# A ViT tower with sparse attention and a product-key FFN: the FFN over one row of tokens in steps of 256, its hot columns, weights and rows all built on VectorE

## The reference

```python
q = (x @ Wq + bq).reshape(-1, N_HEADS, D_KEYS)          # 8 heads, two halves of 64
s1 = jnp.einsum('bhc,hnc->bhn', q1, keys[:, 0])          # 64 keys a half
s1t, i1 = lax.top_k(s1, TOP_K)                           # TOP_K = 8, and the same for s2
all_scores = s1t[..., :, None] + s2t[..., None, :]       # 8 x 8 pairs
scores, best = lax.top_k(all_scores, TOP_K)
indices = take_along_axis(i1 * 64 + i2, best)            # 8 of 4096 experts a head
inner = einsum('bd,bhkd->bhk', x, w_down[indices])
vals = relu(inner) * softmax(scores)
out = einsum('bhk,bhkd->bd', vals, w_up[indices])
```

## Time and profile before

| | us |
|---|---|
| median of 3 runs | 11114.34 (11099.82 to 11156.61) |
| profiled execution, its own time | 11131.57 |
| its span, first to last instruction | 11129.7 |
| mean granted TensorE clock | 0.746 of full |

### The profile page before, as it was taken

How to read it: one execution, slowest core, us unless ns; L and a number is a source line. 1 busy time by engine, 2 the same in 40 slices (tenths; PEclk the granted TensorE clock), 3 DMA queues, 4 the chain that set the end, 5 groups by cost and what they waited for, 6 DMA issues and landing times. The chain is left out here.

```text
span 11129.7 us, 231365 instructions
## 1 busy us (share of the span) xinstructions
PE 8355.6 (75%) x80373; PEld 6346.6 (57%) x80373; DVE 7817.8 (70%) x28721; ACT 3211.1 (29%) x6909; POOL 3313.1 (30%) x2904
## 2 busy tenths in 40 slices
PE   7777767776777677772777777688888888888883
PEld 7555545554555455552555554577777777777773
DVE  2555545555555455557999998888888888888983
ACT  0333333333333333332444444111111111111110
POOL 0111111111111111113444444344444444444441
PEclk8777767776777677776888888677777777777776
DMA  5333333333222333330000000000000000000000
GB/s 154 36 36 36 36 39 36 36 36 39 34 32 33 39 36 36 36 36 2 1 1 1 1 1 1 21 2 2 2 2 2 2 2 2 2 2 2 2 2 24
DMA packets 308211, 234.82 MB, mean 21 GB/s; under 512 B 34770, under 2 KB 305909, under 8 KB 306904
## 3 DMA queue, kind: packets, MB, share of 16 engines
q1 hardware_dynamic: 307224, 222.91, 14.5%
HBM read 48.28 MB, written 6.49 MB: 5 GB/s over the span
## 5 line engine op out<-in xcount | busy, mean ns | idle before, releaser
L1643 POOL TENSOR_TENSOR f_hotp<-f_hotc,f_part 128x1152 bf16<-128x1152 bf16 x579 | 1610.2, 2812 | 1557.0 <-DVE f_hotc L1555 1529.3
L617 DVE TENSOR_REDUCE negmax<-PAIR 99x4 f32<-99x788 f32 x1088 | 1064.5, 978 | 1191.6 <-PE PAIR L373 1052.2
L373 PE MATMUL PAIR<-ks,qs 96*99 96x198 bf16 x4352 | 815.2, 329 | 673.8 <-DVE negmax L617 565.3
L373 PEld LDWEIGHTS PAIR<-ks,qs 96*99 96x99 bf16 x4352 | 540.4, 167 | 1105.7 <-DVE negmax L617 864.6
L528 ACT ACTIVATE probs<-PAIR 99x792 f32<-99x792 f32 x1024 | 851.0, 831 | 1022.5 <-PE PAIR L383 1021.8
L1385 PE MATMUL f_OT<-f_act,f_wu 128*128 128x198 f32 x4096 | 865.5, 378 | 74.9 <-DVE f_act L1581 74.9
L1364 PE MATMUL f_AA<-f_hotp,f_hot 64*128 64x32 bf16 x19584 | 656.2, 236 | 310.3 <-DVE f_act L1581 257.4
L1385 PEld LDWEIGHTS f_OT<-f_act,f_wu 128*128 128x128 f32 x4096 | 831.8, 223 | 83.2 <-DVE f_act L1581 83.2
L383 PE MATMUL PAIR<-qs,ks 99*99 99x198 bf16 x4096 | 765.6, 329 | 124.9 <-ACT probs L528 107.4
L1364 PEld LDWEIGHTS f_AA<-f_hotp,f_hot 64*128 64x128 bf16 x19584 | 626.4, 161 | 342.0 <-DVE f_act L1581 270.0
L1563 DVE TENSOR_TENSOR f_hot<-f_idx,f_iota 128x4608 bf16<-128x4608 bf16 x193 | 804.5, 4168 | 0.0
(11 more groups left out here) (180 smaller groups left out, 15498.6 us busy)
## 6 DMA issues: line engine op xcount, KB each, us to landing
qs<-parts SPq DMA_DIRECT2D x816, 99.0 KB, 4.4
ks<-parts SPq DMA_DIRECT2D x816, 99.0 KB, 6.0
xbuf<-x_in SPq DMA_DIRECT2D x64, 588.0 KB, 4.4
qs<-mrows SPq DMA_DIRECT2D x272, 9.3 KB
out<-h SPq DMA_DIRECT2D x1, 3168.0 KB
out<-h SPq DMA_DIRECT2D x1, 3104.0 KB
wts<-layer_in SPq DMA_DIRECT2D x4, 772.0 KB, 4.2
f_wd<-wdown_in SPq DMA_DIRECT2D x1, 2048.0 KB, 11.0
```

What stands on the lines that cost most here:

```text
L373: mm = nc.tensor.matmul(ps[:, hh, qc * W:qc * W + W], qs[0:STACK, par, 2 * p + hh, j, qc * C:qc * C + C], ks[0:STACK, par, 2 * p + hh, j, ...
L617: V.tensor_reduce(negmax[:, j, :, 2 * p:2 * p + 2].rearrange("p q h -> p h q"), ps[:, :, 0:2 * W].rearrange("p h (q k) -> p h q k", q=2)[: ...
L1643: nc.gpsimd.tensor_tensor(hotp[:, g % 2, pt], hotc[:, g % 2], part[:, pt:pt + 1, t0:t0 + TG].to_broadcast([128, NP, TG]), ALU.mult).then_i ...
```

## The change

The FFN no longer works on h image by image but on one row of 12,672 tokens in DRAM, in 50 steps of 256 (two halves of 128 partitions); the last step begins earlier so that it ends with the row. Attention stores each image to it when it is done (new DMAs on SP's queue); each step loads its 256 rows twice (hx for the statistics and the normalisation, hr for the addition) and stores the sum straight to out. The four stores at the end are gone. h is freed before the FFN, and f_act is double. Four groups of 32 tokens and eight units of 16 replace the groups of 36; VectorE builds hotc (one buffer), all three parts of hotp in one instruction, and hot; GpSimd keeps only deviations. ScalarE normalises. The projection has the tokens as its stationary side, so that its result is in rows and the transposes back are gone; it is in two halves and lies in the next step. inner for the next step lies in pieces between the units of weights; the scores for the step after next likewise, through one PSUM bank (WK), which z and the columns share. In weights the two halves c are now innermost.

```diff
 build_attention, SyncE
+            for n in range(B):
+                upto(sp, added, n, 1)
+                to = tokens[n * W:n * W + W, :]
+                sp.dma_start(to[2:first, :], h[:, n, 0, :]).then_inc(tokens_stored, 16)
+                sp.dma_start(to[first:W, :], h[0:W - first, n, 1, :]).then_inc(tokens_stored, 16)
+                for slot, row in ((C - 2, 1), (C - 1, 0)):
+                    sp.dma_start(to[row:row + 1, :], h[slot:slot + 1, n, 1, :]).then_inc(tokens_stored, 16)
+            sp.wait_ge(tokens_stored, 64 * B)
 build_ffn
-TG = 36
-GROUPS = ((0, 32), (32, 64), (64, C))
+TP = 128
+STEP = 2 * TP
+TG = 32
+GROUPS = TP // TG
 UNIT = 16
+UNITS = TP // UNIT
+    NS = -(-T // STEP)
+    NS += NS % 2
+    at = [min(STEP * n, T - STEP) for n in range(NS)]
...
+        def steps(eng):
+            for n in range(2):
+                yield n, 0, n, n + 1 < NS, n + 2 < NS, n > 0
+            if NS > 4:
+                with eng.Fori(1, NS // 2 - 1) as it:
+                    for par in range(2):
+                        yield it * 2 + par, it, par, True, True, True
+            for n in range(max(NS - 2, 2), NS):
+                yield n, n // 2, n % 2, n + 1 < NS, n + 2 < NS, True
 SyncE
+            def load_x(n):
+                if n >= 2:
+                    upto(sp, z_done, n - 2, 1)
+                    upto(sp, mv_done, n - 2, 1)
+                sp.dma_start(hx[:, n % 2], rows(tokens, n)).then_inc(hx_loaded[n % 2], 16)
+            def load_r(n):
+                if n >= 2:
+                    sp.wait_ge(stored[n % 2], 16 * (n // 2))
+                sp.dma_start(hr[:, n % 2], rows(tokens, n)).then_inc(hr_loaded[n % 2], 16)
...
+            for n in range(NS):
+                load_r(n)
+                if n + 2 < NS:
+                    load_x(n + 2)
+                if n:
+                    store(n - 1)
 TensorE
+            def turn_cols(fr, behind):
+                upto(pe, s_taken, behind, 4)
                 upto(pe, cols_done, fr, 1)
...
+            def weights(n, u):
+                g, slot = u // 2, u % 2
                 upto(pe, hot_done, n, g + 1)
+                upto(pe, aa_taken[slot], n, u // 2)
+                for t in range(UNIT):
+                    tt = slot * UNIT + t
+                    for pt in range(3):
                         for c in range(2):
-                            for pt in range(3):
...
+            def project(n, par, c):
+                if c == 0:
                     for i in range(2):
                         upto(pe, aa_taken[i], n, aa_taken[i].per)
                     upto(pe, added, n, 0)
+                for k in range(NP):
+                    mm = nc.tensor.matmul(OT[:, c * DIM:c * DIM + DIM], act_in[:, par, k, c * TP:c * TP + TP], wu[:, k, :],
+                                          start=(k == 0), stop=(k == NP - 1))
...
+            for n, pair, par, has1, has2, behind in steps(pe):
+                for u in range(UNITS):
+                    if behind and u < 2:
+                        project(n - 1, 1 - par, u)
+                    weights(n, u)
+                    if has2:
+                        if u == 2:
+                            turn_z(n + 2)
+                        elif 3 <= u < 7:
+                            scores(n + 2, par, u - 3)
+                    if has1 and u == UNITS - 1:
+                        turn_cols(n + 1, n + 2 if has2 else n + 1)
+                    if has1 and u >= 2:
+                        first = (0, 2, 5, 8, 10, 13, 16)
+                        inner(n + 1, 1 - par, range(first[u - 2], first[u - 1]))
+            project(NS - 1, (NS - 1) % 2, 0)
+            project(NS - 1, (NS - 1) % 2, 1)
 VectorE
+            def hot_group(n, par, g):
+                t0 = g * TG
+                upto(dve, hotp_done, n, g)
+                V.tensor_tensor(hotc[:, 0], idx[:, par, 1:2, t0:t0 + TG].to_broadcast([128, NP, TG]), iota[:, 0:NP, :],
+                                ALU.is_equal).then_inc(hotc_done.sem, 1)
                 if g >= 2:
+                    upto(dve, aa_ready[1], n, g - 1)
+                elif not isinstance(n, int) or n > 0:
+                    upto(dve, aa_ready[1], n - 1, g + 3)
+                dve.sem_inc(spare, 1)
+                upto(dve, hotc_done, n, g + 1)
+                V.tensor_tensor(hotp[:, g % 2], hotc[:].to_broadcast([128, 3, NP, TG]),
+                                part[:, par, :, t0:t0 + TG].rearrange("p (k o) t -> p k o t", o=1).to_broadcast([128, 3, NP, TG]),
+                                ALU.mult).then_inc(hotp_done.sem, 1)
+                V.tensor_tensor(hot[:, g % 2], idx[:, par, 0:1, t0:t0 + TG].to_broadcast([128, 128, TG]), iota[:],
                                 ALU.is_equal).then_inc(hot_done.sem, 1)
```

More of the change, by code:

```diff
@@ L1193, in build_ffn @@
[L1193 to L1213, removed]
+        hx = sb("f_hx", [TP, 2, 2, DIM])
@@ L1214, in build_ffn @@
+        esum = sb("f_esum", [TP, 2, SEG])
+        idx = sb("f_idx", [128, 2, 2, TP], BF16)
+        part = sb("f_part", [128, 2, 3, TP], BF16)
+        rest = sb("f_rest", [128, 2, TP])
+        hotc = sb("f_hotc", [128, 1, NP, TG], BF16)
+        WK = bank("f_WK")
         IN = [bank(f"f_IN{i}") for i in range(2)]
-        AA = [bank(f"f_AA{i}") for i in range(2)]
+        AA = [[bank(f"f_AA{s}{c}") for c in range(2)] for s in range(2)]
         OT = bank("f_OT")
-        BK = OT[:, 256:512]
@@ L1225, in build_ffn @@
+        hr_loaded = [sem(f"f_hr_loaded{p}") for p in range(2)]
+        stored = [sem(f"f_stored{p}") for p in range(2)]
         dve_step = Count(sem("f_dve_step"), 16)
@@ new lines, in weigh @@
+            def weigh(n, par, u):
+                slot, t0 = u % 2, u * UNIT
+                if u == 0:
+                    upto(dve, inner_taken, n, NP // 2)
+                upto(dve, aa_ready[slot], n, u // 2 + 1)
+                for c in range(2):
+                    sl = act_in[:, par, :, c * TP + t0:c * TP + t0 + UNIT]
+                    last = V.tensor_tensor(sl, sl, AA[slot][c][:].rearrange("p (t n) -> p n t", n=NP), ALU.mult)
+                last.then_inc(aa_taken[slot].sem, 1)
@@ new lines, in _ @@
+            best_keys(0, 0)
+            met(0)
+            key_numbers(0, 0, segs)
+            pair_up(0)
+            for stage in (best_pairs, pair_numbers, ranks):
+                stage(0)
+            numbers_at_ranks(0, 0)
+            add_up(0, 0)
+            places(0)
+            split_cols(0, 0)
+            hot_group(0, 0, 0)
+            assert n_step[0] == dve_step.per, n_step
+            for n, pair, par, has1, has2, behind in steps(dve):
+                fr, other = n + 1, 1 - par
+                if has2:
+                    dve.wait_ge(hx_loaded[par], pair * 16 + 32)
+                    statistics(n + 2, par)
+                hot_group(n, par, 1)
+                if has1:
+                    best_keys(fr, other)
+                weigh(n, par, 0)
+                if has1:
+                    met(fr)
+                    key_numbers(fr, other, segs[:16])
+                weigh(n, par, 1)
+                hot_group(n, par, 2)
+                if behind:
+                    dve.wait_ge(hr_loaded[other], pair * 16 + 16 * par)
+                    add_back(n - 1, other)
+                if has1:
+                    key_numbers(fr, other, segs[16:])
+                    pair_up(fr)
+                weigh(n, par, 2)
+                if has1:
+                    best_pairs(fr)
+                weigh(n, par, 3)
+                hot_group(n, par, 3)
+                if has2:
+                    copy_scores(n + 2, par, 0)
+                if has1:
```

488 lines of the change are left out of this document (226 added, 262 removed).

## The result

| | before | changed |
|---|---|---|
| median, us | 11127.33 (4 runs, 11099.82 to 11156.61) | 10595.88 (4 runs, 10547.1 to 10633.82) |
| ratio, 95% interval | | 0.952 (0.9464 to 0.9575) |
| profiled execution, its span | 11131.57, 11129.7 | 10547.1, 10545.3 |

The account below looks back on a forecast made before the run. VectorE was taken to bound the old loop, TensorE close behind. Steps between 67.9 and 77.1 us were set at 73; 7177 + 48 x 73 gave span 10,681, then + 2 - 17 = 10,665 us, 4.0% faster; range 10,370 to 10,960.

Parts of the forecast that it names:

- VectorE's hot groups: VectorE building f_hotc, f_hotp and f_hot, four groups a step: 4.7 us each, 18.8 together.
- VectorE's sum: All VectorE work in a step of 256 rows, own pauses included: 61.2 us.
- the head: Step's start, through weighing unit 1 at 28.8 us: VectorE has 22.1 us of work and waits 6.7 for TensorE.
- The restart: TensorE's idle at the FFN loop's restart, 3.83 us every second step: 1.9 us a step.
- Small matmuls: TensorE's 96 weights matmuls a unit: 3.15 us, 25.2 for eight units, no effect from alternating halves; ends 12.4 either way.
- The rival on faster alternating matmuls: In weights, alternating halves hide half the weight load: 1.55 us less a unit, about 10,275 us; chance 0.15.
- The clock: TensorE's clock in the FFN loop falls at about every second unit; step between 67.9 (high) and 77.1 us (low).
- P: Period of one FFN step: 73 us expected, between 67.9 and 77.1; span = 7177 + 48 P.
- The bound: FFN step: VectorE bounds at 67.9 us if TensorE's clock stays high; low all through, TensorE's work makes it 77.1.
- A score bank passed back and forth: Single PSUM bank for scores exchanged between TensorE and VectorE: named with the clock's falls for 73 us, no separate price.
- Stores and frame: Start and end around the loop: 166 us of final stores go, one 128 KB store remains; span = 7177 + 48 P.
- the rival on the stores: Steps gain nothing a row, only the end stores' 150 us or so: 10,975 us; within a case given 0.12.

Follow-up runs that it names:

- e14: Changed kernel with 36-element f_hot/f_hotp rows, earlier score copy, inner pieces between units 1 and 2, four steps a loop turn: 10317.49 us, ratio 0.928.
- e1: Changed kernel with the halves c put back outside the three parts in weights: 10604.74 us, ratio 0.953.
- e3: Kernel before, with the halves c made innermost in weights: 11126.05 us, ratio 0.9997.
- e2: Changed kernel with f_hot and f_hotp rows laid out at 36 elements, 32 used (72 bytes apart): 10517.27 us, ratio 0.9442.
- e6: Changed kernel with the third bf16 part of the weights left out of TensorE's small matmuls: 10435.97 us, ratio 0.9394.
- e10: Changed kernel with 36-element f_hot and f_hotp rows, and a score copy moved ahead of hot_group 3: 10375.97 us, ratio 0.9317.
- e4: Kernel before, with out stored image by image during the FFN instead of at the end: 10976.21 us, ratio 0.9851.
- e12: Changed kernel with rows of 36 elements (72 bytes) in f_hot alone: 10527.27 us, ratio 0.9465.
- e15: Changed kernel with rows of 64 elements (128 bytes) in f_hot alone: 11311.79 us in a single run, beside one of 11117.19.

## Why the prediction was right, and where its terms were off

The time (10,665 forecast, 10,596 measured) and the sign came out as said. By its steps:

- **VectorE's hot groups**: right. f_hot 2.28 against 2.2, f_hotp 1.76 against 1.67, f_hotc 0.68 against 0.6: 4.72 a group, as the 4.7 taken. The bf16 price of f_hotp holds and the 3.3 us at the f32 rate does not. The Trainium skill, VectorE: DVE Perf Modes (The perf-mode tier table), had it on that side too, and the trace agrees: 3072 elements in 1758 ns.
- **VectorE's sum**: 61.2 with pauses; busy is 2322.8/2800 x 70.77 = 58.7, and its idle time apart from the waits for units and scores is 2.0: 60.7, within 0.5. But e14 runs at 65.73, under the 67.9 that I gave as VectorE's bound at the high clock, so that bound was 2 us too high, most of it in the head: e14 has 4.7 us of waits for units a step where I had 6.7.
- **The restart**: 1.9 us a step taken from one turn of the kernel before; 1.2 measured (49.3 us in the 2800), and 0.8 in e14 with its four steps a turn.
- **The head**: right in kind and nearly in size. VectorE waits 7.89 us at unit 1 where 6.7 was worked out, and 9.7 a step in all: a unit of 3.60 delays the weighings behind it too.
- **Small matmuls, 3.15 us a unit, "I take no effect"**: mis-sized, and for a reason that was not on my list. I looked at the order, with ends of 12.4 us on either side, and e1 and e3 show that it has no effect. What changed the pace was the padding that TG = 32 took away: 8 x 0.45 = 3.6 us a step. The rival on faster alternating matmuls is gone with e1 and e3. The Trainium skill, TensorE: Matmul & The Clock Gate (Part 3: Packing small matmuls), lets a weight load overlap where the row group differs; these runs show no gain from it for 64-row halves, since 96 matmuls take the same time with the halves changing at each and at every third (254 and 253 ns on the mean, the changed kernel and e1).
- **The clock, "falls at about every second unit"**: mis-sized the other way. The count was right, 12 of 21; the price wasn't, as the clock is mostly back within the stretch. TensorE's busy time is 69.2 us a step; less the 3.6, it stands at 65.6 between my 58.5 (high) and 88.4 (low), a quarter of the way. I had set P at 73, over half way from 67.9 to 77.1. With 3.15 us a unit e2 has 69.80, so this term, with the restart in it, was some 3 us a step too dear, and the pace, 1.0 to 1.6 net of the wait that it hid, was too cheap. Two errors of opposite sign left 2.2, or 69 us of time where the clock's term alone would have left about 150: that the forecast came so near is in part luck.
- **The bound**: I said that VectorE bounds if the clock is high and TensorE if it is low. TensorE is busy 98% at 0.86, and bounds it, with the exchange of the score bank close behind.
- **A score bank passed back and forth**: named in half a sentence, with no price. It is small as long as TensorE is slow (0.3 us a step), and the next link once it isn't (e2, e6, e10).
- **Stores and frame**: right. The last store lies within 2.7 us of the last addition, and e4 puts the 166 us at 166, which is also the rival on the stores at 10,975 against 10,976 measured. The formula gives 10,574 for P = 70.77, 29 above the span: start and end together were put that much too long.

## What to carry to other kernels

When a tile's shape changes, look at the spacing of the operand that TensorE loads, not only at its element count: a padding that looks like waste may be what makes it fast. When an engine is freed and the time follows only by a part, ask the waits of the new trace before judging the edit: here 3.6 us a step showed as 1.0 to 1.6 until one copy was moved. Two kernels that are equally fast gave periods 1.0 us apart in their profiles: a small gain is read from several executions, not from one trace. Work given to GpSimd beside VectorE's large bf16 instructions should be priced with what they lose meanwhile.

## What the runs showed of the hardware

- A 64 x 128 stationary load in bf16 with a 64 x 32 matmul is paced at 32.5 ns with the columns 72 bytes apart, 37.5 at 64 bytes and 49 at 128 bytes (e12, the changed kernel, e15).
- The slowest pace goes with a lower granted clock over the loop, 0.76 in e15 for 0.86 in the changed kernel, with TensorE busy 99% and 98%, and with longer f32 matmuls (543 ns for 469). One run shows it, and not why.
- VectorE's bf16 compare of 4608 elements takes 2.55 us without GpSimd beside it and 4.15 with it; with the one of 1152 elements (1.11 for 0.75) VectorE's two instructions of a group lose 1.96 us, as much as the f_hotp that GpSimd takes off it costs there (1.95).
- A loop turn costs TensorE some 2.5 us in the changed kernel (49.3 us in about 20 turns; 1.52 and 2.70 in the two above) in which it waits for nothing that the trace shows, and 3.83 in the turn of the earlier trace rows.
